# Adapter packs laid out by batch and loaded with eight broadcast loads a block; order of splits in the attention loop changed

## The chip, the cores and the metric

One Trainium2 chip, one core of it, one launch. The time is device microseconds of that core. Every multiplication is done on TensorE (PE); VectorE (DVE), ScalarE (ACT) and GpSimd (POOL) do the elementwise work; SyncE (SP) issues most of the DMA transfers.

## The reference, cut to what matters

Eight sequences of 128 tokens with 512 features, float32, go through four residual blocks. Every sequence (batch entry) b has its own adapter number, so low-rank weights are picked by number at run time.

```
x = x + einsum('bsi,boi->bso', x, W0[lora_ids])                      # block 0: a full matrix per batch entry
# block 1: attention, 32 query heads, 8 key/value heads, head dim 128, rank R = 16
lora_linear(x, w, a, b) = x @ w + (x @ a[ids]) @ b[ids]               # ids = attn_ids
q, k, v = rope(lora_linear(x, wq, aq, bq)), rope(lora_linear(x, wk, ak, bk)), lora_linear(x, wv, av, bv)
p = softmax(q k^T / sqrt(128), causal and masked);  o = p v
x = x + lora_linear(o, wo, ao, bo)
# blocks 2 and 3: rank-16 adapters and one dense 512x512 matrix with bias
```

## The kernel before, in words

Float32 products are made of three matmuls on rounded parts: high x high, high x low, low x high, where high = the value rounded by ScalarE (`ACT.Copy` into the fp32r type) and low = value - high, computed by DVE or POOL. An adapter product needs only rank 16, so the high and low parts are stacked on the partition axis and one matmul with 128 rows does it: for a pair of batch entries the stack holds 4 quarters of 32 rows, each quarter with 16 rows of the even and 16 rows of the odd entry. The "pack" (weight side, `pack0`, `pack1`, written in `split_pieces`, L430, and `low_pieces`, L519) has the high part in partitions 0 to 63 and the low part in 64 to 127. The activation side (`axn`, then transposed to `axt_all`) has high, low, high, low.

The raw rows of a pack come by `load_block_b` (L176): for each of the 8 batch entries SP reads the adapter number into a register and issues 4 loads of 16 rows x 512 columns (32 KB), one for each quarter, 32 loads a block. Five blocks (v 0, v 1, k 0, k 1, and the first query block) are made ahead of the attention loop; the first query block comes from `bq_sel`, a DRAM copy gathered by POOL (L628), by `load_rows` (L180), 4 loads. In the loop `load_bq` (L190) reads the next head's rows, 4 loads for each half.

Phase 1 ("steps" s, 0 to 37, one instruction stream per engine written out by hand): step s does PE `values(s-2)` of block v, `product(s)` of block 0, `adapters(s-1)` and `turn_x1(s)`; ACT and DVE split what these need, in the order of the code. From step 18 on the 16 key units (k) and 4 query units (q) follow: PE `project`, DVE the two rotation products (L609, L611), POOL their sum (L668), SP the store into `k_rot`. PIECES says at which step each piece of a weight block (w) or pack (b) is split. SP's order is one list: x, a, w0 loads of the steps with the block loads between them; a load waits in that list until its buffer is free, and all behind it wait too. `a_raw` has 3 buffers.

Phase 2, the attention loop: 8 key/value heads x 8 slots (one batch entry each). PE in a slot: `scores`, `turn`, `queries`, `outputs` of the entry before last, `values` of the last. In slot 1 of a head ACT makes the 4 high parts of the output weights (`wo_hi`, order 0, 2, `ot`, 1, 3). DVE makes low parts 0 (end of slot 1) and 1 (in slot 2, before the reciprocal), L1004; POOL makes low parts 2 and 3 and that of `ao` (L976, L979). DVE makes the low part of the query pack in every odd slot before the reciprocal (L999). POOL scales the probabilities (L966) and sums the rotation (L959), PE needs the sums of slots 3 and 7 for the scores behind them.

Phase 3, from about 785 us on: blocks 2 and 3.

Of the kernel before, what the change touches and what calls it, by code (L numbers as in the profile page):

```python
# [7 lines left out]
P = 128  # L8
# [18 lines left out]
R_PACK = 16  # L27
# [3 lines left out]
def program(nc, x, xt, lora_ids, pos, attn_ids, slot_ids, mask, w0, wq, wk, wv, wo, a3, bq, bk, bv, ao, bo,  # L31
            l2a, l2b, w3, b3, l3a, l3b, ident_c, causal_c, rope_c, gather_c, twin_c, out):
# [20 lines left out]
    bq_sel = nc.dram_tensor("bq_sel", (B, R, KVH * GW), F32, kind="Internal").ap()  # L53
# [10 lines left out]
    with whole:  # L64
# [30 lines left out]
        twin = sb(whole, "twin", [P, 3])  # L95
        l2b_sel = sb(whole, "l2b_sel", [P, KC, B, R])
# [28 lines left out]
        axn = [sb(early, f"axn{i}", [P, 3, 4, 2, R], F32R) for i in range(2)]  # L125
# [9 lines left out]
        raw_b_in = sem(attn, "raw_b_in")  # L135
# [47 lines left out]
        RAW_B_IN = (512, 1024, 1536, 2048, 2048 + 64)  # L183

# [20 lines left out]
        with ExitStack() as c:  # L205
            for i in (1, 2):
# [5 lines left out]
            RAW = 3  # L212
# [7 lines left out]
                     for flat, at in ((l2a_flat, 0), (l2a_flat, 3 * KC * R), (l2b_flat, 0))]  # L220
# [65 lines left out]
            with nc.Block() as block:  # L286
                @block.sync
                def _(sp):
# [3 lines left out]
                    def load_a(b):  # L292
                        pick = sp.value_load(id_rows[0:1, 1, b:b + 1], min_val=0, max_val=a3.shape[0] - 1)
                        if b >= RAW:
                            sp.wait_ge(a_lo_done, b - RAW + 1)
                        sp.dma_start(a_raw[b % RAW].rearrange("p c n r -> p (c n r)"),
# [24 lines left out]
                    load_block_b(sp, 0)  # L321
                    load_x(1)
                    load_a(1)
                    load_w0(2)
                    load_x(2)
                    load_a(2)
                    for b in range(RAW, B):
                        load_w0(b)
                        load_x(b)
                        load_a(b)  # L330
                        if b == 5:
                            sp.wait_ge(w_lo_done, KC)
                            load_block_w(sp, 1)
                        if b == 6:
                            sp.wait_ge(b_lo_done, PAIRS)
                            load_block_b(sp, 1)
                    sp.wait_ge(b_lo_done, 2 * PAIRS)
                    load_block_b(sp, 2)
# [5 lines left out]
                    load_block_b(sp, 3)  # L344
                    for m in range(VU):
# [29 lines left out]
                def _(act):  # L375
# [21 lines left out]
                    def split_a(b):  # L397
# [3 lines left out]
                        act.activation(a_hi[b % 2][:, :, :, :], a_raw[b % RAW], ACT.Copy).then_inc(a_hi_done, 1)  # L401

                    def pack_hi(b):
# [5 lines left out]
                        act.activation(axn[i][:, :, 0:4:2, i, :], ps_a.unsqueeze(2).broadcast_to([P, 3, 2, R]), ACT.Copy).then_inc(axn_hi_done, 1)  # L409
# [5 lines left out]
                    def split_pieces(s):  # L415
                        for j, kind, k in PIECES.get(s, []):
# [9 lines left out]
                            else:  # L426
                                act.wait_ge(raw_b_in, RAW_B_IN[j])
# [14 lines left out]
                    act.dma_start(ident[:, :], ident_c).then_inc(consts_in, 16)  # L442
                    split_xt(0)
                    split_w0(0, 0, KC)
                    act.wait_ge(consts_in, 16)
# [37 lines left out]
                def _(dve):  # L483
                    low = slice(P // 2, P)
# [19 lines left out]
                    def pack_lo(b):  # L504
                        i = b % 2
                        dve.wait_ge(axn_hi_done, b + 1)
                        dve.tensor_tensor(axn[i][:, :, 1:4:2, i, :], ps_a.unsqueeze(2).broadcast_to([P, 3, 2, R]),
# [1036 lines left out]
```

## Time and profile before

| | us |
|---|---|
| median of 3 runs | 848.53 (847.76 to 848.71) |
| the profiled execution | 849.5 |
| its span in the profile | 847.8 |
| PE busy in the span | 755.8 (89%) |
| DVE, ACT, POOL busy | 536.1, 324.8, 294.1 |
| mean granted clock of PE | 0.956 |

In the rows of the profile a time is the start in us from the begin of the span, then the duration. `SPq` and `ACTq` are the instruction queues that issue transfers. `[16.16 <-DVE res L497]` behind a row means that the engine sat idle for 16.16 us before it and that this wait ended with the named instruction. "x4" merges four instructions into one row.

### The profile page before, as it was taken

The page shows a single profiled execution, that of the slowest core. Times are in us where ns is not written, and L with a number is a line of the kernel's source. Part 1 is how long each engine was busy: PE and PEld are TensorE (multiplying, and loading weights), DVE is VectorE, ACT ScalarE, POOL GpSimd, SP SyncE. Part 2 cuts the span into 40 slices and gives each one's busy share as a digit, 9 for nine tenths or more (in the row PEclk, how much of TensorE's full clock was granted, in tenths as well). Part 3 has the DMA queues.
Part 4 walks back from the last instruction along what each step waited for, and adds up shares of the span by engine and source line. Part 5 has one row for each costly group of instructions (what it writes and reads, how often), then busy time and mean ns, then how long its engine had stood idle before and what let it go on. Part 6 is the DMA issues. An engine that isn't in the chain of part 4 may idle for free. (4 is left out here: it accounts for less than half of the span.)

```text
span 847.8 us, 13367 instructions
## 1 busy us (share of the span) xinstructions
PE 755.8 (89%) x4100; PEld 623.1 (73%) x4100; DVE 536.1 (63%) x1370; ACT 324.8 (38%) x902; POOL 294.1 (35%) x265
## 2 busy tenths in 40 slices
PE   3292989879779999999999999999999999998798
PEld 2282877657567887887887888788788788876586
DVE  3251558756866667657566667666765756654883
ACT  4261525112053435335344435343534533433550
POOL 1020325253545236235326335423623532420220
PEclk8587899989889999999999999999999999999899
DMA  6573678546604122303303302312130310620502
GB/s 218 215 267 94 193 239 269 157 157 191 215 9 137 39 63 66 109 16 108 111 0 108 127 0 62 136 38 62 65 108 21 103 37 0 151 26 2 128 14 87
DMA packets 63083, 87.88 MB, mean 104 GB/s; under 512 B 20086, under 2 KB 37654, under 8 KB 59334
## 3 DMA queue, kind: packets, MB, share of 16 engines
q1 hardware_dynamic: 44338, 73.54, 28.0%
q10 hardware_dynamic: 17044, 8.46, 3.3%
q0 software_dynamic: 1664, 5.44, 2.1%
q8 instruction: 17, 0.28, 0.1%
q14 instruction: 20, 0.16, 0.1%
HBM read 72.45 MB, written 19.68 MB: 109 GB/s over the span
## 5 line engine op out<-in xcount | busy, mean ns | idle before, releaser
L966 POOL TENSOR_TENSOR prob<-prob,rinv 128x512 f32<-128x512 f32 x64 | 66.6, 1040 | 255.3 <-DVE rinv L1054 255.3
L907 ACT ACTIVATE ot_hi<-ps_o 128x512 fp32r<-128x512 f32 x64 | 38.1, 595 | 222.1 <-PE ps_o L1110 222.1
L1122 PE MATMUL ps_out<-wo_hi,ot_hi 128*128 128x512 f32 x256 | 102.8, 402 | 10.4 <-DVE wo_lo L1004 5.7
L959 POOL TENSOR_TENSOR qt<-qc,qs 128x512 f32<-128x512 f32 x60 | 77.9, 1298 | 70.0 <-DVE qs L993 70.0
L917 ACT ACTIVATE prob<-sm,nmax 128x128 f32<-128x128 f32 x256 | 99.8, 392 | 6.2 <-DVE nmax L1035 4.5
L1123 PE MATMUL ps_out<-wo_lo,ot_hi 128*128 128x512 f32 x256 | 101.3, 396 | 0.0
L1124 PE MATMUL ps_out<-wo_hi,ot_lo 128*128 128x512 f32 x256 | 100.8, 394 | 0.0
L78 PE MATMUL ps_q<-x1t_hi,wgt_hi 128*128 128x512 f32 x240 | 100.4, 418 | 0.0
L80 PE MATMUL ps_q<-x1t_hi,wgt_lo 128*128 128x512 f32 x240 | 95.4, 398 | 0.0
L79 PE MATMUL ps_q<-x1t_lo,wgt_hi 128*128 128x512 f32 x240 | 95.2, 397 | 0.0
L1032 DVE MEMSET gate<- 128x1 f32 x64 | 3.8, 59 | 136.9 <-PE ps_s L1091 136.9
L993 DVE TENSOR_TENSOR qs<-ps_q,trig 64x512 f32<-64x512 f32 x120 | 82.6, 689 | 3.7
L1091 PEld LDWEIGHTS ps_s<-kt,qt 128*128 128x128 f32 x512 | 66.6, 193 | 17.5 <-issue 10.3
L1091 PE MATMUL ps_s<-kt,qt 128*128 128x128 f32 x512 | 69.9, 280 | 7.5 <-PEq L286 6.8
L1122 PEld LDWEIGHTS ps_out<-wo_hi,ot_hi 128*128 128x128 f32 x256 | 48.2, 188 | 24.8 <-DVE wo_lo L1004 9.2
L1035 DVE CUSTOM_DVE_ANT_0 sm<-ps_s,maskbias 128x128 f32<-128x128 f32 x256 | 59.1, 286 | 0.9 <-issue 0.2
L1124 PEld LDWEIGHTS ps_out<-wo_hi,ot_lo 128*128 128x128 f32 x256 | 48.0, 187 | 11.6
L901 ACT ACTIVATE pt_hi<-ps_t 128x512 fp32r<-128x512 f32 x64 | 38.2, 596 | 44.1 <-PE ps_t L1100 44.1
L1123 PEld LDWEIGHTS ps_out<-wo_lo,ot_hi 128*128 128x128 f32 x256 | 48.3, 188 | 8.1
L80 PEld LDWEIGHTS ps_q<-x1t_hi,wgt_lo 128*128 128x128 f32 x240 | 45.4, 189 | 10.7
L78 PEld LDWEIGHTS ps_q<-x1t_hi,wgt_hi 128*128 128x128 f32 x240 | 45.8, 191 | 8.0
L79 PEld LDWEIGHTS ps_q<-x1t_lo,wgt_hi 128*128 128x128 f32 x240 | 45.7, 190 | 8.1
(193 smaller groups left out, 1720.2 us busy)
## 6 DMA issues: line engine op xcount, KB each, us to landing
raw_w<-in_wq SPq DMA_DIRECT2D x8, 1024.0 KB, 5.3
wo_raw<-in_wo SPq DMA_DIRECT2D x8, 1024.0 KB, 4.9
raw_b<-bq_sel SPq DMA_DIRECT2D x56, 128.0 KB, 5.2
qt<-in_w SPq DMA_DIRECT2D x5, 1024.0 KB, 6.8
v_hi_d<-v_hi ACTq DMA_DIRECT2D x16, 256.0 KB, 4.6
v_lo_d<-v_lo ACTq DMA_DIRECT2D x16, 256.0 KB, 5.1
kt<-k_rot SPq DMA_DIRECT2D x16, 256.0 KB, 2.6
v_hi<-v_hi_d SPq DMA_DIRECT2D x16, 256.0 KB, 3.2
```

Source lines behind the costliest of these rows:

```text
L78: pe.matmul(bank[:, :], w_hi[:, k, cols], x1t_hi[:, k, tok], start=(k == 0), stop=False)
L79: pe.matmul(bank[:, :], w_hi[:, k, cols], x1t_lo[:, k, tok], start=False, stop=False)
L80: pe.matmul(bank[:, :], w_lo[:, k, cols], x1t_hi[:, k, tok], start=False, stop=False)
L917: e = act.activation(prob[i][:, h, :], sm[:, h, :], ACT.Exp, bias=nmax[i][:, h:h + 1], scale=-1.0, accum_out=rsum[i][:, h:h + 1])
L959: pool.tensor_tensor(qt[:, half, h, :], qc[:, :], qs[:, :], ALU.add).then_inc(q_done, 1)
L966: pool.tensor_tensor(prob[i][:, :, :], prob[i][:, :, :], rinv[i][:, :].unsqueeze(2).broadcast_to([P, G, T]), ALU.mult).then_inc(prob_done, 1)
L993: dve.tensor_tensor(qs[to:to + 64, :], ps_q[i][at:at + 64, :], sin_t[to:to + 64, tok], ALU.mult).then_inc(q_mult, 1)
L1035: m = dve.tensor_tensor_reduce(out=sm[:, h, :], in0=ps_s[i][:, h, :], in1=maskbias[:, b, :], scale=-1.0, scalar=3.0e38, op0=ALU.add, op1=A ...
L1091: mm = pe.matmul(ps_s[b % 2][:, h, :], qt[:, half, h, at:at + T], kt[:, b * T:(b + 1) * T], start=True, stop=True)
L1122: pe.matmul(ps_out[:, :], ot_hi[:, q], wo_hi[:, h, :], start=(h == 0), stop=False)
L1123: pe.matmul(ps_out[:, :], ot_hi[:, q], wo_lo[:, h, :], start=False, stop=False)
L1124: pe.matmul(ps_out[:, :], ot_lo[:, q], wo_hi[:, h, :], start=False, stop=(h == G - 1))
```

## The change

1. Packs are laid out by batch entry: entry b of a pair has partitions 64 (b%2) to 64 (b%2) + 63, in four copies of its 16 rows. One load with a source that repeats four times fills 64 rows (128 KB), so a block takes 8 loads instead of 32. Loads of a pair have their own semaphore.
2. The low part is no longer taken on half of the partitions: one `scalar_tensor_tensor` over 128 partitions computes raw - high where a column of constants (`lows`) is -1 and raw where it is 0. `lows` is one more small constant load on ACT's queue.
3. SP's list: the loads of v block 0 are spread over the steps (pair 0 behind x and a of step 1, pair 1 behind step 2, pairs 2 and 3 behind step 3). `a_raw` has a fourth buffer.
4. `bq_sel` is stored by head, so the gather writes 8 runs of 32 KB per entry.
5. Loop: ACT makes `wo_hi` 0 to 3 in order ahead of `ot`; DVE makes only low part 0, POOL 1, 2 and 3; DVE's query pack low part comes behind the rotation products.

```diff
-    bq_sel = nc.dram_tensor("bq_sel", (B, R, KVH * GW), F32, kind="Internal").ap()
+    bq_sel = nc.dram_tensor("bq_sel", (KVH, B, R, GW), F32, kind="Internal").ap()
...
-        axn = [sb(early, f"axn{i}", [P, 3, 4, 2, R], F32R) for i in range(2)]
+        axn = [sb(early, f"axn{i}", [P, 3, 2, 4, R], F32R) for i in range(2)]
...
-        def load_block_b(dma, j):
+        def load_block_b(dma, j, pairs):
             src = (bv, bv, bk, bk)[j]
             cols = slice(j % 2 * GW, (j % 2 + 1) * GW)
-            for b in range(B):
+            for b in range(2 * pairs[0], 2 * pairs[-1] + 2):
                 pick = dma.value_load(id_rows[0:1, 1, b:b + 1], min_val=0, max_val=src.shape[0] - 1)
-                for quad in range(4):
-                    at = 32 * quad + R * (b % 2)
-                    dma.dma_start(raw_b[at:at + R, b // 2, :], src[bass.DynSlice(pick, 1), :, cols].rearrange("a r n -> (a r) n")).then_inc(raw_b_in, 16)
+                four_times(dma, b, src[bass.DynSlice(pick, 1), :, cols], raw_b_in[b // 2])
+
+        def four_times(dma, b, rows, done):
+            dma.dma_start(raw_b[4 * R * (b % 2):4 * R * (b % 2 + 1), b // 2, :], rows.broadcast_to([4, R, GW])).then_inc(done, 16)
...
         def load_bq(dma, g, h):
-            for quad in range(4):
-                dma.dma_start(raw_b[32 * quad:32 * quad + 32, 2 * h:2 * h + 2, :],
-                              bq_sel.rearrange("(c two) r n -> (two r) c n", two=2)[:, 2 * h:2 * h + 2, bass.DynSlice(g * GW, GW)]
-                              ).then_inc(bq_in[h], 16)
+            for b in range(HALF * h, HALF * (h + 1)):
+                four_times(dma, b, bq_sel[bass.DynSlice(g, 1), b], bq_in[h])
...
                     load_block_w(sp, 0)
-                    load_block_b(sp, 0)
                     load_x(1)
                     load_a(1)
+                    load_block_b(sp, 0, range(0, 1))
                     load_w0(2)
                     load_x(2)
                     load_a(2)
+                    load_block_b(sp, 0, range(1, 2))
                     for b in range(RAW, B):
                         load_w0(b)
                         load_x(b)
                         load_a(b)
+                        if b == 3:
+                            load_block_b(sp, 0, range(2, 4))
...
                             sp.wait_ge(gathered, 2 * B * 16)
-                            load_rows(sp, raw_b, bq_sel[:, :, 0:GW], raw_b_in)
+                            for b in range(B):
+                                four_times(sp, b, bq_sel[0:1, b], raw_b_in[b // 2])
...
-                                act.wait_ge(raw_b_in, RAW_B_IN[j])
+                                act.wait_ge(raw_b_in[k], 32 * (j + 1))
...
-                                dve.tensor_tensor(pack[low, k, :], raw_b[low, k, :], pack[low, k, :].bitcast(F32), ALU.subtract).then_inc(b_lo_done, 1)
+                                dve.scalar_tensor_tensor(pack[:, k, :], pack[:, k, :].bitcast(F32), lows[:, 0:1], raw_b[:, k, :],
+                                                         ALU.mult, ALU.add).then_inc(b_lo_done, 1)
...
-                        pool.dma_start(bq_sel[b:b + 1], bq[pick]).then_inc(gathered, 16)
+                        pool.dma_start(bq_sel[:, b], bq[pick].rearrange("a r (g n) -> (a g) r n", n=GW)).then_inc(gathered, 16)
...
-                        sp.wait_ge(wo_lo_done, G // 2 * (g + 1))
-                        sp.wait_ge(wo_lo_pool, G // 2 * (g + 1))
+                        sp.wait_ge(wo_lo_done, g + 1)
...
-                                wo_hi_part(g, 0)
-                                wo_hi_part(g, 2)
+                                for h in range(G):
+                                    wo_hi_part(g, h)
                             if not first or b >= 1:
                                 ot(t - 1, None if not first else t - 1)
                             if b == 1:
-                                wo_hi_part(g, 1)
-                                wo_hi_part(g, 3)
                                 ao_hi_part(g)
...
-                                for h in range(G // 2, G):
-                                    pool.wait_ge(wo_hi_done, G * g + 2 * (h - G // 2) + 2)
+                                for h in range(1, G):
+                                    pool.wait_ge(wo_hi_done, G * g + h + 1)
                                     pool.tensor_tensor(wo_lo[:, h, :], wo_raw[:, h, :], wo_hi[:, h, :].bitcast(F32),
                                                        ALU.subtract).then_inc(wo_lo_pool, 1)
...
                                 pt(t - 1)
-                            if b == 2:
-                                wo_lo_part(g, 1)
-                            if not last and b % 2:
-                                bq_lo_part(PAIRS * g + b // 2 + 1, b // 2)
                             dve.wait_ge(exp_done, t + 1)
...
                             if not (last and b >= HALF):
                                 rotate(t, (b // HALF + 1) % 2, i)
+                            if not last and b % 2:
+                                bq_lo_part(PAIRS * g + b // 2 + 1, b // 2)
                             if b == 1:
                                 wo_lo_part(g, 0)
```

## Rows read from the trace of the kernel before

**Rows 1.** Page: granted clock of PE in 40 slices of 21.2 us.

```profile
PEclk8587899989889999999999999999999999999899
```

**Rows 2.** Timeline of PE, startup: gaps, and one matmul at either clock.

```profile
41.41 1.12 PE L693 MATMUL ps_x<-ident,res 128*128 128x128 f32 x4 [16.16 <-DVE res L497]
...
85.91 0.90 PE L716 MATMUL ps_ax<-ident_r,axn 128*128 128x128 f32 x3 [16.42 <-DVE axn L507]
...
182.65 0.77 PE L78 MATMUL ps_p<-x1t_hi,wgt_hi 128*128 128x512 f32 x1 [4.89 <-DVE pack L519]
183.21 0.63 PE L79 MATMUL ps_p<-x1t_lo,wgt_hi 128*128 128x512 f32 x1
...
188.71 0.40 PE L80 MATMUL ps_p<-x1t_hi,wgt_lo 128*128 128x512 f32 x1
...
214.97 0.77 PE L78 MATMUL ps_p<-x1t_hi,wgt_hi 128*128 128x512 f32 x1 [2.92 <-DVE pack L519]
```

**Rows 3.** Timeline of SP's queue, startup.

```profile
8.25 1.38 SPq L166 DMA_DIRECT2D raw_w<-in_wv  x1
10.37 19.34 SPq L176 DMA_DIRECT2D raw_b<-in_bv  x32
...
32.43 0.34 SPq L310 DMA_DIRECT2D trig<-in_w  x1
...
63.14 19.05 SPq L176 DMA_DIRECT2D raw_b<-in_bv  x32
...
155.88 19.70 SPq L176 DMA_DIRECT2D raw_b<-in_bk  x32
175.64 0.42 SPq L348 DMA_DIRECT2D k_rot<-l2a_sel  x1
...
202.27 1.83 SPq L180 DMA_DIRECT2D raw_b<-bq_sel  x4
```

**Rows 4.** Timelines of ACT, DVE and POOL, startup.

```profile
20.40 2.18 ACT L425 ACTIVATE wgt_hi<-raw_w 128x512 fp32r<-128x512 f32 x4
37.31 2.00 ACT L391 ACTIVATE wgt_hi<-trig 128x1024 fp32r<-128x1024 f32 x2 [2.27 <-DMA trig<-in_w]
38.40 2.36 DVE L491 TENSOR_TENSOR wgt_lo<-trig,wgt_hi 128x1024 fp32r<-128x1024 f32 x2 [5.87 <-ACT wgt_hi L391]
83.61 0.63 ACT L430 ACTIVATE pack<-raw_b 128x512 fp32r<-128x512 f32 x1 [18.42 <-DMA raw_b<-in_bv]
177.93 1.55 POOL L668 TENSOR_TENSOR l2a_sel<-qt 128x512 f32<-128x512 f32 x1 [13.49 <-DMA k_rot<-l2a_sel]
209.70 2.19 ACT L430 ACTIVATE pack<-raw_b 128x512 fp32r<-128x512 f32 x4 [16.04 <-DMA raw_b<-bq_sel]
```

**Rows 5.** Tile raw_b: durations in ns, min/median/max.

```profile
L176 SPq DMA_DIRECT2D raw_b<-in_bv x64: 315/365/373, 10.4 to 81.8; - x64
L190 SPq DMA_DIRECT2D raw_b<-bq_sel x56: 332/377/768, 225.3 to 657.5; - x56
L999 DVE TENSOR_TENSOR pack<-raw_b,pack x28: 689/689/1472, 247.1 to 710.1; 64x512 fp32r<-64x512 f32 x28
```

**Rows 6.** Busy time by stretch: us, PE PEld DVE ACT POOL, clock, DMA share, GB/s.

```profile
10.00:15.00 5.00, 3.21 (x9) 2.16 (x7) 0.69 (x1) 1.72 (x4) 1.27 (x1) 1.00 0.99 408
140.00:160.00 20.00, 15.01 (x59) 11.75 (x58) 17.72 (x23) 7.83 (x13) 5.47 (x6) 0.91 0.89 276
```

**Rows 7.** Timelines of PE and POOL, slots 1 to 3 of the second head.

```profile
318.64 1.05 PE L1091 MATMUL ps_s<-kt,qt 128*128 128x128 f32 x8
...
328.16 1.05 PE L1091 MATMUL ps_s<-kt,qt 128*128 128x128 f32 x8
...
336.64 1.16 PE L1091 MATMUL ps_s<-kt,qt 128*128 128x128 f32 x8
...
319.89 3.00 POOL L976 TENSOR_TENSOR wo_lo<-wo_raw,wo_hi 128x512 fp32r<-128x512 f32 x2
```

**Rows 8.** PE's wait for the low parts of the output weights, whole span.

```profile
PE ps_out L1122 <- DVE wo_lo L1004: 5.7, 8, 0.9
```

More of the change, by code:

```diff
@@ L31, in program @@
 def program(nc, x, xt, lora_ids, pos, attn_ids, slot_ids, mask, w0, wq, wk, wv, wo, a3, bq, bk, bv, ao, bo,
-            l2a, l2b, w3, b3, l3a, l3b, ident_c, causal_c, rope_c, gather_c, twin_c, out):
+            l2a, l2b, w3, b3, l3a, l3b, ident_c, causal_c, rope_c, gather_c, twin_c, lows_c, out):
     B, T, HID = x.shape
@@ L95, in program @@
         twin = sb(whole, "twin", [P, 3])
+        lows = sb(whole, "lows", [P, 1])
         l2b_sel = sb(whole, "l2b_sel", [P, KC, B, R])
@@ L134, in program @@
         raw_w_in = sem(attn, "raw_w_in")
-        raw_b_in = sem(attn, "raw_b_in")
+        raw_b_in = [sem(attn, f"raw_b_in{p}") for p in range(PAIRS)]
         wq_in = sem(attn, "wq_in")
@@ L219, in program @@
             a_raw = [flat[:, at:at + 3 * KC * R].rearrange("p (c n r) -> p c n r", c=KC, n=3)
-                     for flat, at in ((l2a_flat, 0), (l2a_flat, 3 * KC * R), (l2b_flat, 0))]
+                     for flat, at in ((l2a_flat, 0), (l2a_flat, 3 * KC * R), (l2b_flat, 0), (l2b_flat, 3 * KC * R))]
             kr = [l2a_flat, l2b_flat]
@@ L335, in _ @@
                             sp.wait_ge(b_lo_done, PAIRS)
-                            load_block_b(sp, 1)
+                            load_block_b(sp, 1, range(0, 4))
                     sp.wait_ge(b_lo_done, 2 * PAIRS)
-                    load_block_b(sp, 2)
+                    load_block_b(sp, 2, range(0, 4))
                     sp.wait_ge(w_lo_done, 2 * KC)
@@ L343, in _ @@
                     sp.wait_ge(b_lo_done, 3 * PAIRS)
-                    load_block_b(sp, 3)
+                    load_block_b(sp, 3, range(0, 4))
                     for m in range(VU):
@@ L400, in split_a @@
                             act.wait_ge(ax_ready, b - 1)
-                        act.activation(a_hi[b % 2][:, :, :, :], a_raw[b % RAW], ACT.Copy).then_inc(a_hi_done, 1)
+                        act.activation(a_hi[b % 2][:, :, :, :], a_raw[b % AR], ACT.Copy).then_inc(a_hi_done, 1)
                     def pack_hi(b):
@@ L408, in pack_hi @@
                             act.wait_ge(axt_ready, b - 1)
-                        act.activation(axn[i][:, :, 0:4:2, i, :], ps_a.unsqueeze(2).broadcast_to([P, 3, 2, R]), ACT.Copy).then_inc(axn_hi_done, 1)
+                        act.activation(axn[i][:, :, i, 0:4:2, :], ps_a.unsqueeze(2).broadcast_to([P, 3, 2, R]), ACT.Copy).then_inc(axn_hi_done, 1)
                     def copy_axt(b):
@@ L483, in _ @@
                 def _(dve):
-                    low = slice(P // 2, P)
                     steps = [0]
@@ L579, in _ @@
                     split_w0(0, 0, KC)
+                    dve.wait_ge(consts_in, 32)
                     for s in range(LAST):
@@ L997, in bq_lo_part @@
                         dve.wait_ge(bq_hi_done, n)
[L998 to L1000 removed]
+                        dve.scalar_tensor_tensor(bq_pack[:, p, :], bq_pack[:, p, :].bitcast(F32), lows[:, 0:1], bq_raw[:, p, :],
+                                                 ALU.mult, ALU.add).then_inc(bq_lo_done, 1)
                     def wo_lo_part(g, h):
[L1003 removed]
+                        dve.wait_ge(wo_hi_done, G * g + h + 1)
                         dve.tensor_tensor(wo_lo[:, h, :], wo_raw[:, h, :], wo_hi[:, h, :].bitcast(F32), ALU.subtract).then_inc(wo_lo_done, 1)
@@ L1117, in outputs @@
                             q = slice(h * T, (h + 1) * T)
-                            if b == 0 and h < G // 2:
-                                pe.wait_ge(wo_lo_done, G // 2 * g + h + 1)
+                            if b == 0 and h == 0:
+                                pe.wait_ge(wo_lo_done, g + 1)
                             elif b == 0:
-                                pe.wait_ge(wo_lo_pool, G // 2 * g + h - G // 2 + 1)
+                                pe.wait_ge(wo_lo_pool, (G - 1) * g + h)
                             pe.matmul(ps_out[:, :], ot_hi[:, q], wo_hi[:, h, :], start=(h == 0), stop=False)
@@ L1523, in constants @@
     gather = np.stack([(row % R_PACK == col % R_PACK) & (col // R_PACK % 2 == i) for i in range(2)], 1).astype(np.float32)
-    return {"ident_c": np.eye(P, dtype=np.float32), "causal_c": causal, "rope_c": rope, "gather_c": gather, "twin_c": twin}
+    lows = np.where(np.arange(P)[:, None] % (4 * R_PACK) >= 2 * R_PACK, -1.0, 0.0).astype(np.float32)
+    return {"ident_c": np.eye(P, dtype=np.float32), "causal_c": causal, "rope_c": rope, "gather_c": gather, "twin_c": twin, "lows_c": lows}
 def kernel(**inputs):
```

24 lines of the change are left out of this document (10 added, 14 removed).

## The prediction

> **What bounds the kernel now.** I first read the slices of the page. In the attention loop PE is at 90% or more of every slice and its granted clock is at the upper level; in the first quarter of the span the clock digits fall to 5 and 7 [rows 1]. So the startup (0 to 237 us) has waits of PE that cost twice, once as idle time and once as slow matmuls behind them. PE's timeline shows them: 16.16 us idle before 41.41, 16.42 before 85.91, 4.89 before 182.65, 2.92 before 214.97 [rows 2]. Behind 182.65 the same matmul takes 0.63 us where it takes 0.40 later: 1.2 GHz against 2.4 GHz [rows 2]. Next I asked what SP's queue was doing in these gaps: it was issuing the 32 small loads of an adapter block, for 19.34 us from 10.37, for 19.05 us from 63.14 and for 19.70 us from 155.88 [rows 3]. ACT waits 18.42 us for the second of these blocks (until 83.61), POOL 13.49 us for a k_rot store that stands behind the third, ACT 16.04 us for the first query pack [rows 4]. These loads move 1 MB in 19 us where the DMA engines do 408 GB/s when asked [rows 6]; the issuing, not the moving, takes the time. Of the loop I read slots: 8.48 us from 328.16 to 336.64, but 9.52 from 318.64 to 328.16 [rows 7], the slot in which PE waits for DVE's second low part of the output weights, 8 times in all [rows 8].
>
> **Step 1, the issue time of a block.** One load issues in 0.365 us, and 128 KB loads issue in 0.377 [rows 5], so size does not price it. Per batch entry SP spends 19.34/8 = 2.42 us: four issues of about 0.42 and 0.74 for the register load, as much as lies between the end of raw_w's issue (9.63) and 10.37 [rows 3]. New: 0.74 + 0.42 = 1.16 per entry, 9.3 us a block, 10 less. Bounds of one new issue: 0.33 to 0.77 [rows 5]; I take the median.
>
> **Step 2, the first gap.** PE's wait before 41.41 ends with DVE's addition for step 1, which stands behind DVE's split of w0(2), which waits for the load issued at 32.43 [rows 2 to 4]. New list between raw_w (9.63) and that issue: x(1) 0.4, a(1) 1.1, two pack loads 2.3, register and xt 1.1: issue at about 14.6 instead of 32.43. The DMA engines are full until then, so it lands at some 20 to 23 (1.3 MB at 408 GB/s is 3.2 us, behind 0.5 MB of others). That is in time for ACT, which is busy with the four pieces of raw_w until 22.6 [rows 4]. From there: pack piece 0.6, xt 0.6, two w0 pieces 2.0 (as at 37.31), so 25.8; DVE ends its half 1.45 us after ACT, as 40.76 against 39.31 [rows 4], 27.2; addition 0.7: PE starts at 27.9 instead of 41.41. **13.5 us**. Of the slow matmuls behind the gap (11 x 0.2 us) about half should go, as a gap of 2.7 us stays: **1.0**. Bounds 11 to 15.7.
>
> **Step 3, the second gap.** The second block can't begin earlier than its buffer is free, so everything up to it moves with step 2. ACT needed pair 0 at 65.2 on the old clock of the trace and got the whole block at 83.61 [rows 4]. New: pairs have own semaphores; the loads of pair 0 issue at 63.1 and 64.3 [rows 3], those of pair 1 until 67.0, and land 2 to 5 us later. ACT is then 2 to 6 us late; PE, which could go on until 69.5 (85.91 less 16.42, rows 2), waits 1.6 to 6 us. I take 3.9 us of gap left and 1 us of slow clock instead of 2: 16.4 - 3.9 + 1.0 = **13.5 us**. Bounds 11 to 17.
>
> **Step 4, the v blocks (87 to 155 us).** No gain, no loss. Here DMA is at 0.89 of its time [rows 6] (v stores, gathers), and what ends the waits of ACT is the landing of stores. The change moves no bytes away. It makes the gather of bq write 32 KB runs from 2 KB rows. Bounds: 3 us won, 10 us lost.
>
> **Step 5, the k and q units.** The block issued at 155.88 ends after 9.4 instead of 19.7 us, the store of 175.64 goes out at 165.3, and POOL's wait of 13.49 us shrinks to some 3 [rows 3, 4]. PE has work until 177.8 (182.65 less 4.89), so its gap of 4.89 goes, with 9 slow matmuls behind (1.8 us) and two small stalls after it, 1.9 us as I estimate them. The query pack: issued in 8 x 0.42 = 3.4 us instead of 1.83, but used by pair, so the first pairs come at about the old time; relative to PE, which has won 8.6 us by then, SP's list has won 10.3. The gap of 2.92 goes (and some 2.6 us of slow matmuls, as the clock fell behind it too) [rows 2], sum 14.2. I give 2.7 back: the k_rot stores behind the eight loads land later, and POOL waits for these. **11.5 us**; bounds 6 to 15.
>
> **Step 6, the loop.** PE's extra in slot 2's start is 9.52 - 8.48 = 1.04 us, 8 times, 8.3 us; the row of waits itself says 5.7 [rows 7, 8]. DVE's second low part goes; POOL makes three at 1.5 us each, from 319.9 to 324.4 [rows 7], and `ao` until 325.7. PE, without its stall, needs them at 323.7, 324.4, 325.1 and 325.8: they are in time by 0.1 to 2 us, the last one barely. Then the move of DVE's query low part: the reciprocal and the rotation products come up to 0.7 us earlier in odd slots, and the low part (0.69 us, when against POOL up to 1.47 [rows 5]) now runs beside POOL's rotation sum, on whose end PE's scores wait in slots 4 and 0. The first brings 0.3 us (the products wait for PE's queries), the second costs up to 0.4; 0 to -0.1 net, 15 times, so -1.3. The new low part on 128 instead of 64 partitions costs the same, since a row of 512 elements sets it. **7.0 us**; bounds 2 to 9.5.
>
> By the Trainium skill (SBUF — State Buffer, on the shared port pair) a DVE instruction with two SBUF inputs and a POOL instruction that reads SBUF exclude each other for their whole length. The 1472 ns maximum beside the 689 ns median fits that [rows 5]. By that rule alone each of the 15 meetings would cost the full 0.7 us less the 0.3 won, 6 us, and step 6 would bring 2.
>
> **Small things.** One more constant load on ACT's queue (0.4 us) lies in ACT's wait for the first weights. Three instead of two pieces of POOL in slot 1 end before its next scaling is wanted by PE (328). Phase 3 is untouched.
>
> **Sum.** 14.5 + 13.5 + 0 + 11.5 + 7.0 = 46.5 us. The profiled execution took 849.5, so 803.0; the median is 1.0 lower than that execution, so 802 us.
>
> **The rivals.**
>
> A, the broadcast loads use few DMA engines. If a load whose outermost dimension is the fourfold copy runs on 4 of the 16 engines, 128 KB take 131072/(408/4 GB/s) = 1.28 us [rows 6], a block 10.3 us on these four, and every transfer behind it waits for them. Block 0 is still hidden but for 1 us of step 2. In step 3 pair 1 lands some 3 us later: another 2.5 us. In step 5 the query pack takes 10.3 us and the stores behind it as long: 2.5 more. Time 802 + 6 = 808. For it: nothing in this trace has such a shape, and nothing speaks against it. The Trainium skill (DMA: Bandwidth & Descriptors, the section on why a DMA increments its semaphore by 16) says the count of engines is the largest up to 16 that divides the outermost non-1 sizes of both sides, and its table of mistakes names the leading broadcast; no row here shows it.
>
> B, the v stretch takes back what came earlier: with DMA at 0.89 there, the denser startup leaves a backlog, and the gather in smaller pieces is slower. The bounds of step 4 price it: 10 us, 812. For it: that share. Against it: the two gaps before 87 us are stretches in which DMA does little but these small loads, so the denser startup fills them.
>
> C, slower than before: rival A's four engines, not hidden. Each of the five startup blocks would hold all transfers behind it for 10.3 - 2.6 = 7.7 us, 38 us, and each of the 14 half packs of the loop for 3.8, 53 us, when PE waits for the transfer behind. It decides from 46.5 us on; with all of the startup and 15 us of the loop exposed it gives 802 + 53 = 855. Against it: in the loop a pack has over 60 us before its use.
>
> D, the change doesn't do what it says: the broadcast load issues as slowly as four (0.42 x 4). Then only the new order gains: step 2 some 10, step 6's 7, the pair semaphores 8: 824.
>
> **Chances.** Forecast 0.55, A 0.22, B 0.12, D 0.07, C 0.03; 0.01 for no change. About 0.2% (1.7 us) is what a measurement can tell here. Faster 0.95, same 0.02, slower 0.03. The forecast's own range is 794 to 810; with the best bounds of all steps (15.7 + 17 + 3 + 15 + 9.5 = 60) it would be 789. For 8 in 10 I reach to B and a part of D: 788 to 821.
>
> **What would show it.** Step 1: `raw_b` loads 8 a block, spaced 1.16 us. Step 2: the second `turn_x1` of PE at 28 instead of 41.4. Step 3: a gap of 2 to 6 us before the fourth `turn_ax`. Step 4: the time from there to the last v unit unchanged. Step 5: no PE wait for `pack` over 1.5 us in the k units, store of the first k_rot 10 us after the block's first load. Step 6: slot 2 of a head as long as slot 3, no wait of L1122 for `wo_lo`. Rival A: landing of a pack load over 3 us at an idle DMA, and DMA share low while loads queue. Wrong would be: a v stretch longer by over 10 us, a new wait of PE for POOL in every head, or a gap before 41 us still over 8 us.

## The result, and the profile after

| kernel | median, us | ratio to before [95%] |
|---|---|---|
| before | 848.62 | |
| after | 827.13 (824.06 to 828.97) | 0.974 [0.970, 0.978] |

The change made the kernel 21.5 us faster, where 46.5 us were forecast. The profiled execution took 826.34 us, its span is 824.7. Behind the start of the loop it gave what it should (7.9 us, 7.0 forecast); of the startup's 39.5 us only 15.2 came.

Timeline of PE after, its longest gaps of the startup behind the first steps and the first scores of the loop:

```profile
29.66 1.12 PE L698 MATMUL ps_x<-ident,res 128*128 128x128 f32 x4 [6.26 <-DVE res L500]
...
66.29 0.90 PE L721 MATMUL ps_ax<-ident_r,axn 128*128 128x128 f32 x3 [3.96 <-DVE axn L510]
...
137.94 0.76 PE L78 MATMUL ps_p<-x1t_hi,wgt_hi 128*128 128x512 f32 x1 [4.18 <-DVE pack L522]
...
163.55 0.47 PE L78 MATMUL ps_p<-x1t_hi,wgt_hi 128*128 128x512 f32 x1 [1.80 <-DVE pack L522]
...
203.58 0.77 PE L78 MATMUL ps_p<-x1t_hi,wgt_hi 128*128 128x512 f32 x1 [8.28 <-DVE pack L522]
...
221.74 2.05 PE L1090 MATMUL ps_s<-kt,qt 128*128 128x128 f32 x8 [6.83 <-PEq L285]
```

The two gaps of 16 us are now 6.26 and 3.96, so the order of SP's list does what it should there. But the wait ahead of the query units (of their second, the first that needs all four pieces of the pack) has grown from 2.92 us to 8.28, and the one in front of the second key unit from 3.37 (154.72 in the kernel before) to 4.18. Both end with a low part of a pack. So I read who waits for packs: ACT's high parts of the first query pack, as in the last row of [rows 4].

```profile
187.32 0.63 ACT L433 ACTIVATE pack<-raw_b 128x512 fp32r<-128x512 f32 x1 [13.60 <-DMA raw_b<-bq_sel]
190.05 0.63 ACT L433 ACTIVATE pack<-raw_b 128x512 fp32r<-128x512 f32 x1 [2.10 <-DMA raw_b<-bq_sel]
192.72 0.63 ACT L433 ACTIVATE pack<-raw_b 128x512 fp32r<-128x512 f32 x1 [2.03 <-DMA raw_b<-bq_sel]
195.70 0.63 ACT L433 ACTIVATE pack<-raw_b 128x512 fp32r<-128x512 f32 x1 [2.35 <-DMA raw_b<-bq_sel]
```

SP issued all eight loads between 182.14 and 186.77, 0.58 us apart, yet the pairs land 2.7 to 3.0 us apart: it is no longer the issuing that sets the pace. The table by stretches (columns as in [rows 6]) says what does:

```profile
58.00:63.00 5.00, 4.33 (x28) 3.52 (x26) 2.31 (x4) 0.68 (x2) 0.00 (x0) 1.00 0.27 100
190.00:195.00 5.00, 5.00 (x24) 4.10 (x23) 1.83 (x3) 1.26 (x2) 0.00 (x0) 1.00 0.26 90
```

In these stretches hardly anything but pack loads is under way, ACT waits for them, and still the DMA engines are busy for a quarter: 90 to 100 GB/s, a quarter of the 408 of [rows 6]. That is rival A.

ACT has the last high part at 196.33, but PE starts only at 203.58. What lies between is a k_rot store that SP issued behind the eight loads. It lands 9.4 us later; POOL waits for it, DVE waits for POOL, and DVE's last two low parts stand behind that in its order. The rows are those of SP's queue, POOL and DVE; the last one is the same wait of POOL behind the key block, 13.49 us in [rows 4]:

```profile
186.82 0.49 SPq L350 DMA_DIRECT2D k_rot<-l2b_sel  x1
196.33 1.26 POOL L673 TENSOR_TENSOR l2b_sel<-qt 128x512 f32<-128x512 f32 x1 [8.94 <-DMA k_rot<-l2b_sel]
197.70 0.69 DVE L614 TENSOR_TENSOR qt<-ps_p,trig 128x512 f32<-128x512 f32 x1 [5.80 <-POOL l2b_sel L673]
...
199.86 0.75 DVE L522 SCALAR_TENSOR_TENSOR pack<-pack,lows,raw_b 128x512 fp32r<-128x512 f32 x1
...
202.68 0.75 DVE L522 SCALAR_TENSOR_TENSOR pack<-pack,lows,raw_b 128x512 fp32r<-128x512 f32 x1
...
158.84 1.28 POOL L673 TENSOR_TENSOR l2a_sel<-qt 128x512 f32<-128x512 f32 x1 [10.29 <-DMA k_rot<-l2a_sel]
```

PE was idle from 195.30. With the low part (0.75 us) right behind ACT's last high part it could have gone on at some 197.1, so by this estimate the landing of the pack itself makes about 1.8 of the 8.28 us, and the store behind it the rest.

SP's queue after, then its loads of the k blocks (duration in ns: minimum, median, maximum), then two rows of the DMA issues (the last number is the median from issue to landing):

```profile
11.50 2.68 SPq L179 DMA_DIRECT2D raw_b<-in_bv  x2
...
15.82 0.35 SPq L309 DMA_DIRECT2D trig<-in_w  x1
```

```profile
L179 SPq DMA_DIRECT2D raw_b<-in_bk x16: 615/616/621, 76.6 to 152.2; - x16
```

```profile
qt<-in_w SPq DMA_DIRECT2D x5, 1024.0 KB, 10.5
...
trig<-in_w SPq DMA_DIRECT2D x2, 1024.0 KB, 11.4
```

The third w0 is issued at 15.82 (forecast 14.6, before 32.43). It lands 9.7 us later where it took 4.8 before, at a time when the DMA engines are full (share 1.00 from 12 to 17 us), and PE's row that answers to 41.41 comes at 29.66 and not at 27.9. The 11.4 us is the median of two w0 loads; the other one, issued at 37.1, takes 13.2 us.

### The profile page after: what moved, and what is told of

It reads as the page before. It is cut to its first block and busy times, and to the rows that moved or that the text cites. A ratio compares the mean times of both kernels' runs of the same rounds, so it can differ in the third digit from the quotient of the medians.

```text
span 824.7 us, 13217 instructions
## 1 busy us (share of the span) xinstructions
PE 752.7 (91%) x4100; PEld 624.8 (76%) x4100; DVE 542.7 (66%) x1362; ACT 324.0 (39%) x902; POOL 313.8 (38%) x273
## 5 line engine op out<-in xcount | busy, mean ns | idle before, releaser
L962 POOL TENSOR_TENSOR qt<-qc,qs 128x512 f32<-128x512 f32 x60 | 84.2, 1404 | 78.0 <-DVE qs L995 78.0
L1123 PEld LDWEIGHTS ps_out<-wo_hi,ot_lo 128*128 128x128 f32 x256 | 48.0, 187 | 11.5
L993 DVE TENSOR_TENSOR qc<-ps_q,trig 128x512 f32<-128x512 f32 x60 | 41.4, 690 | 21.2 <-PE ps_q L83 21.2
L78 PE MATMUL ps_p<-x1t_hi,wgt_hi 128*128 128x512 f32 x80 | 35.0, 438 | 18.9 <-DVE pack L522 18.9
## 6 DMA issues: line engine op xcount, KB each, us to landing
qt<-in_w SPq DMA_DIRECT2D x5, 1024.0 KB, 10.5
```

The costliest lines, as they stand in the source:

```text
L78: pe.matmul(bank[:, :], w_hi[:, k, cols], x1t_hi[:, k, tok], start=(k == 0), stop=False)
L962: pool.tensor_tensor(qt[:, half, h, :], qc[:, :], qs[:, :], ALU.add).then_inc(q_done, 1)
L1123: pe.matmul(ps_out[:, :], ot_lo[:, q], wo_hi[:, h, :], start=False, stop=(h == G - 1))
```

## The experiments

Each kernel was timed against the kernel before on the same chip; before took 848.6 to 850.4 us on the chips used. The column of the first scores is the start of the loop in the span of the profiled execution.

| kernel | engines a load | loads a v/k block | median, us | ratio [95%] | first scores |
|---|---|---|---|---|---|
| before | 16 | 32 | 848.62 | | 236.91 |
| after | 4 | 8 | 827.13 | 0.974 [0.970, 0.978] | 221.74 |
| rows outermost | 16 | 8 | 802.23 | 0.945 [0.942, 0.947] | 196.87 |
| small loads | 16 | 32 | 829.65 | 0.976 [0.972, 0.979] | 226.13 |
| two copies | 2 | 16 | 861.24 | 1.013 [1.009, 1.018] | 253.33 |
| old order | 16 | 8 | 807.98 | 0.952 [0.948, 0.956] | 199.89 |
| small rows | 16 | 32 | 842.66 | 0.992 [0.990, 0.994] | 236.06 |
| early packs | 16 | 8 | 798.47 | 0.940 [0.935, 0.945] | 192.19 |
| early packs, again | 16 | 8 | 802.49 | 0.946 [0.943, 0.948] | 188.26 |
| rows outermost, again | 16 | 8 | 803.32 | 0.945 [0.942, 0.948] | 196.12 |
| loop only | 16 | 32 | 843.19 | 0.992 [0.989, 0.994] | |
| output weights only | 16 | 32 | 843.07 | 0.992 [0.990, 0.995] | |

"Engines a load" is rival A's count for the v and k blocks, the outermost extent of the load's rows; it is the thing under test. The query packs of small loads and two copies stay those of the change (4).

**Rows outermost** puts the 16 rows and not the four copies first in source and destination. Bytes, count and order of the loads are those of the change.

```diff
-rows.broadcast_to([4, R, GW])
+rows.rearrange("a r n -> (a r) n").unsqueeze(1).broadcast_to([R, 4, GW])
...
-    lows = -1 where p % 64 >= 32
+    lows = -1 where p % 4 >= 2        # and axn [P, 3, 2, R, 4]
```

> The changed kernel with another order of the rows in a pack: the four copies of a row lie side by side, so the repeating dimension of a load's source is inside the 16 rows and not outside them. Same bytes, same 8 loads a block, same instructions elsewhere. Theory (few engines): in the changed kernel a pack load runs on 4 of 16 DMA engines. Its rows: 90 GB/s at a DMA share of 0.26 from 190 to 195 us, when only pack loads are under way, and pairs that reach ACT 2.7 us apart (190.05, 192.72) although two loads issue in 1.2 us. Then here: pairs land under 1.5 us apart, the issue of a load falls from 0.62 to 0.4 us, the gaps of PE before 66.3, 137.9 and 203.6 shrink by 15 to 20 us in all, total 806 to 814. Rival (issue): SP's queue takes its time for any load of 64 rows, wherever the repetition stands; then issue stays 0.62, total 825 to 829. Rival (DMA-bound startup): bytes decide, total 822 to 829 with a faster landing.

It took 802.23 us, 25 us less than the change and even below the 806 to 814 expected. Two details missed: an issue lasts 0.55 us and not 0.4, and the three gaps named shrink by 7.4 us together (3.96, 4.18 and 8.28 to 0.17, 5.33 and 3.48), not by 15 to 20. The rest came from smaller waits and from the clock: between the row at 29.66 (28.12 here) and the first scores PE is busy for 146.9 us instead of 156.4 for the same matmuls, at a granted clock of 0.96 instead of 0.89. ACT's high parts of the first query pack, the same four as above:

```profile
164.96 0.63 ACT L433 ACTIVATE pack<-raw_b 128x512 fp32r<-128x512 f32 x1 [11.75 <-DMA raw_b<-bq_sel]
166.25 0.63 ACT L433 ACTIVATE pack<-raw_b 128x512 fp32r<-128x512 f32 x1 [0.66 <-DMA raw_b<-bq_sel]
167.45 0.63 ACT L433 ACTIVATE pack<-raw_b 128x512 fp32r<-128x512 f32 x1 [0.57 <-DMA raw_b<-bq_sel]
168.68 0.63 ACT L433 ACTIVATE pack<-raw_b 128x512 fp32r<-128x512 f32 x1 [0.59 <-DMA raw_b<-bq_sel]
```

The pairs come 1.2 to 1.3 us apart, the pace at which SP issues them (5.03 us for the eight). POOL's two waits for k_rot stores, 10.29 and 8.94 us in the change, are 3.90 and 2.54:

```profile
138.19 1.29 POOL L673 TENSOR_TENSOR l2a_sel<-qt 128x512 f32<-128x512 f32 x1 [3.90 <-DMA k_rot<-l2a_sel]
...
169.38 1.29 POOL L673 TENSOR_TENSOR l2b_sel<-qt 128x512 f32<-128x512 f32 x1 [2.54 <-DMA k_rot<-l2b_sel]
```

The other loads of the startup land earlier too:

```profile
qt<-in_w SPq DMA_DIRECT2D x5, 1024.0 KB, 7.8
...
raw_w<-in_wv SPq DMA_DIRECT2D x2, 1024.0 KB, 9.4
raw_b<-in_bv SPq DMA_DIRECT2D x16, 128.0 KB, 3.5
trig<-in_w SPq DMA_DIRECT2D x2, 1024.0 KB, 7.5
```

PE's rows that answer to those of the change, with the 4.18 in front of the second key unit not gone but 5.33:

```profile
55.41 0.55 PE L721 MATMUL ps_ax<-ident_r,axn 128*128 128x128 f32 x3 [0.17 <-DVE axn L510]
...
124.66 0.77 PE L78 MATMUL ps_p<-x1t_hi,wgt_hi 128*128 128x512 f32 x1 [5.33 <-DVE pack L522]
...
196.87 2.05 PE L1090 MATMUL ps_s<-kt,qt 128*128 128x128 f32 x8 [6.84 <-PEq L285]
```

**Small loads**: the change, but the four v and k blocks by 32 loads of 16 rows, in the change's order and with semaphores by pair.

```diff
-four_times(dma, b, src[bass.DynSlice(pick, 1), :, cols], raw_b_in[b // 2])
+for q in range(4):
+    at = 4 * R * (b % 2) + q * R
+    dma.dma_start(raw_b[at:at + R, b // 2, :], src[...].rearrange("a r n -> (a r) n")).then_inc(raw_b_in[b // 2], 16)
```

> The changed kernel, but the loads of the four v and k blocks are again 32 of 16 rows each (the query packs keep the broadcast loads); order in SP's list, semaphores by pair and layout stay changed. Few-engines theory: issuing costs 2.4 us an entry again, 19 us a block, but nothing queues on four engines. The first gap stays small (spread order), the second is 8 to 12 us instead of 4, the k blocks as before: total 828 to 838. If the broadcast loads were harmless, the 5.5 us a block that SP loses more here would show as 10 us and more: total 838 to 846.

829.65 us. Against the change (827.13) the intervals of the two ratios overlap: eight loads on four engines are worth about as much as 32 loads on all. The change's gain in the startup is then in the main that of its order, its semaphores and the fourth buffer. Rows outermost is 27 us below it, by fewer issues or by its query packs; the next kernel was to part these.

**Small rows**: rows outermost, with its query packs, and the v and k blocks by 32 loads. In that layout a load of 16 rows writes every fourth partition.

```diff
-four_times(dma, b, src[...], raw_b_in[b // 2])
+for q in range(4):
+    dma.dma_start(raw_b[at + q:at + 4 * R:4, b // 2, :], src[...].rearrange("a r n -> (a r) n")).then_inc(raw_b_in[b // 2], 16)
```

> Rows outermost (802.2 us), but the four value and key blocks by 32 loads of 16 rows each (every fourth partition); the query packs stay eight loads over all 16 engines. It differs from small loads (829.65 us) in the query packs alone, which there come over 4 engines, and from rows outermost in the count of issues alone. Theory: the 27 us between those two are mostly the issue, 19.7 to 21.2 us a block instead of 10.5; the query packs' part is what PE's wait ahead of the query units differs by, 9.37 against 3.48 us, so about 5. Time 821 to 826 us, first scores of the loop near 219. Rival: the issue is hidden by the order and the semaphores by pair, and most of the 27 us came with the query packs; time 803 to 812 us, first scores before 208.

842.66 us, outside both expectations, as the edit changed a thing that it should not. The loads' durations in ns (minimum, median, maximum), first in small rows and then in small loads:

```profile
L177 SPq DMA_DIRECT2D raw_b<-in_bk x64: 495/538/2202, 86.5 to 176.2; - x64
```

```profile
L177 SPq DMA_DIRECT2D raw_b<-in_bk x64: 315/368/671, 74.9 to 159.3; - x64
```

A load of the same 32 KB issues in 0.54 us instead of 0.37 when it writes every fourth partition, so a block takes SP 25.5 to 27.6 us. It does not part issue and query packs cleanly, but it shows the issue by itself: with the same query packs, 16 us more a block cost 40 us, 2.5 us for each. At that rate the 9 to 11 us a block between small loads and rows outermost are some 24 of their 27 us; that is an estimate, and leaves some 3 for the query packs. PE's wait ahead of the query units says more (9.37 us in small loads, 3.48 in rows outermost, 2.38 in small rows), so the split is open by some 3 us. The fewer issues are worth about as much as the four engines cost, and the change gained the one and paid the other.

**Two copies**: the same question from the other side. Each batch's rows come by two loads of two copies each.

```diff
-dma.dma_start(raw_b[64 rows], rows.broadcast_to([4, R, GW]))
+for half in range(2):
+    dma.dma_start(raw_b[32 rows], rows.broadcast_to([2, R, GW]))
```

> The kernel after, but each batch's rows of the four value and key blocks come by two loads of 64 KB that say each [2 copies][16 rows][512], where it has one of [4 copies][16 rows][512]; places in the pack, order and waits by pair stay, and the query packs too. Bytes are the same, and there are 16 loads a block where the kernel with 32 small loads (829.65 us) has 32. Theory (a load runs on as many DMA engines as its outermost count, and the start of every list falls on the same ones): only 2 of the 16 engines carry these 1 MB, so where nothing else is in flight the DMA share falls from 0.26 to about 0.13 and the rate from 90 to 100 GB/s to about 50; a block drains in some 20.5 us instead of 10.3 us. Issue is 16 x 0.6 + 8 x 0.74 = 15.5 us, so from now on the drain and not the issue sets when a block is there. Between rows-outermost (a block drains in about 2.6 us, 802.2 us) and the kernel after (10.3 us, 827.1 us) the startup lost 3.2 us for each us of drain; by that slope it would be 860 us, by a slope that flattens at least 838 us. The wait ahead of the third turn of the adapter rows (3.96 us in the kernel after) grows past 8 us. Rival (a broadcast source costs per load and not by its engines): the share stays near 0.26 and the time between 825 and 832 us.

861.24 us, slower than the kernel before and near the 860 expected. The stretches of the second key block, in which at the end only pack loads are under way:

```profile
170.00:175.00 5.00, 5.00 (x25) 4.05 (x24) 4.64 (x7) 0.63 (x1) 1.72 (x3) 1.00 0.17 62
175.00:180.00 5.00, 5.00 (x25) 4.14 (x24) 0.75 (x1) 0.63 (x1) 0.00 (x0) 1.00 0.13 49
```

A share of 0.13 is 2 of 16, 49 GB/s is half of the change's. PE's wait for the adapter rows (3.96 us at 66.29 in the change) is 10.91:

```profile
81.70 0.90 PE L724 MATMUL ps_ax<-ident_r,axn 128*128 128x128 f32 x3 [10.91 <-DVE axn L513]
```

For the extents 4 and 2 share and rate go with the outermost extent, and for 16, 4 and 2 the time does: 802, 827 and 861 us. Two copies has 16 loads a block instead of 8, so a part of its loss could be issue; but small loads, with 32 and an issue of the same 20 us a block, is 32 us faster. How many engines a load of rows outermost uses no row shows, since SP's issuing sets its pace; 16 is rival A's count.

**Old order**: rows outermost with all eight loads of v block 0 in the place of before.

```diff
+                    load_block_b(sp, 0, range(0, 4))      # ahead of x(1)
-                    load_block_b(sp, 0, range(0, 1))      # and the other two places
```

> Rows outermost, as in the run of 802.2 us, but the first value block's eight loads are all issued where the kernel before issues its 32, ahead of the second batch's x and adapter load and of the third w0; the semaphores by pair stay. It says what the order of the first block is worth once the loads are spread over all engines. SP then issues 8 x (0.74 + 0.55) = 10.3 us in one piece ahead of x of batch 1, where the kernel before issues for 22.06 us and rows-outermost only 2 loads (2.6 us) ahead of the third w0. Theory that the order matters (the loads of batches 1 and 2 are late by what SP issues ahead of them): the turn of x1 of batch 1 comes near 35 us instead of 28.1 us and the third turn of the adapter rows 4 to 8 us later than at 55.4 us; total 806 to 811 us. Rival (once the issue of a block is 10 us, its place is of no account, since the transfers of the startup fill the 16 engines anyway): first turn later, but all made up by the first key unit (119 to 125 us), total 801 to 804 us.

807.98 us: the order is worth some 6 us (ratio 0.952 [0.948, 0.956] against 0.945 [0.942, 0.947]; against the second timing of rows outermost, [0.942, 0.948], the intervals touch). PE turns x1 of batch 1 at 32.12 us (28.12 in rows outermost; expected near 35), and the loop starts 3.0 us later. In the profiled executions another 4 us lie behind the first scores; no wait that I found accounts for them, and executions of one kernel differ by as much.

**Output weights only** and **loop only** put the loop's edits into the kernel before: first the new split of `wo` alone, then with DVE's query low part behind the rotation too (on 64 partitions, as before).

```diff
-                            if not last and b % 2:
-                                bq_lo_part(PAIRS * g + b // 2 + 1, b // 2)
                             dve.wait_ge(exp_done, t + 1)
...
                                 rotate(t, (b // HALF + 1) % 2, i)
+                            if not last and b % 2:
+                                bq_lo_part(PAIRS * g + b // 2 + 1, b // 2)
```

> As the last, but DVE's low part of the query pack stays ahead of the reciprocal. My step 6 gave 8.3 us to the split of the output weights and -1.3 to the move of the low part: then this is 839 to 841, 1 us faster than the one with both. Rival: the move is what takes PE's wait for the rotation sum away at slots 4 and 0 (3 us in the trace of before): then this is 843 to 845.

> The kernel before with only the edits of the attention loop: wo_hi in order, one low part on DVE and three on POOL, the query pack's low part behind the rotation products (still a subtraction on 64 partitions). The changed kernel's heads are 67.5 us apart instead of 68.8. If that is from these edits alone: 840 to 842. Rival (the loop gains because the pack loads or layout changed): 846 to 849.

843.07 us and 843.19 us. By their ratios and the 850 us of before on that chip, 6.5 and 7.2 us are won, each to within 2.3. The move costs nothing that this measurement can tell; the 1.3 us it was charged with are within the error. Of the expectations, loop only lies above its 840 to 842, and output weights only falls into its rival's 843 to 845. That rival has its cause wrong: PE's weight loads wait for the rotation sum for 3.0 and 3.1 us in the two, 3.1 before, so the move takes nothing away.

**Early packs** is a further version, pointed at by the 5.33 us above. In rows outermost ACT's high parts of the first key block stand in steps 15 to 17, each behind a wait for a v store (3.65 us at 119.28). They move to steps 11 to 13.

```diff
-11: [(2, "w", 0)], 12: [(2, "w", 1)], 13: [(2, "w", 2)], ... 15: [(2, "b", 1)], 16: [(2, "b", 2)], 17: [(2, "b", 3)]
+11: [(2, "w", 0), (2, "b", 1)], 12: [(2, "w", 1), (2, "b", 2)], 13: [(2, "w", 2), (2, "b", 3)]
```

> Rows outermost (802.2 us) and one further edit: the low and high parts of the last three pairs of the first key block are taken in steps 11, 12 and 13 instead of 15, 16 and 17, so that they no longer stand behind ScalarE's waits for the v stores (3.65 us at 119.28) and SP can load the second key block some 15 us earlier. Theory: TensorE's wait of 5.33 us at 124.66 (released by VectorE's low part of a pack) goes to under 1.5 us, and ScalarE's four waits for the loads of the second key block at 129.59 to 137.43 (2.99, 2.02, 1.93, 1.98 us) go to under 0.5; total 796 to 799 us. Rival (the wait is taken back at the query blocks, which wait for the table work and the rotation on VectorE, busy for 7.78 of the 8 us from 172 to 180): total 800.5 to 803 us.

798.47 us. ACT and PE:

```profile
127.01 2.18 ACT L433 ACTIVATE pack<-raw_b 128x512 fp32r<-128x512 f32 x4
```

```profile
121.83 0.50 PE L78 MATMUL ps_p<-x1t_hi,wgt_hi 128*128 128x512 f32 x1 [0.58 <-DVE v_lo L597]
...
174.46 0.47 PE L78 MATMUL ps_p<-x1t_hi,wgt_hi 128*128 128x512 f32 x1 [3.51 <-DVE pack L522]
```

The wait of 5.33 is gone, ACT's four pieces of the second key block run without a wait, and the loop starts 4.7 us earlier. As the interval [0.935, 0.945] meets that of rows outermost, I ran both again on one chip.

> The early packs kernel (798.47 us in its first run) once more, five rounds, beside the next kernel on the same chip. If the edit is worth what the start of the loop showed (4.7 us), it is 3 to 6 us below rows outermost here; if the total gained nothing, within 1.5 us of it.

> Rows outermost once more, five rounds, for the direct comparison with early packs on one chip: 800 to 804 us, 3 to 6 us above early packs if that edit shows in the total.

The profiled executions differ as before, first scores at 188.26 against 196.12 and 796.65 us against 804.55, but the medians are 802.49 (796.65 to 806.25) and 803.32 (798.7 to 806.28). The executions of either kernel spread over about 1%, and the total does not show the gain. Both versions beat the change by 24 to 29 us; between them nothing is decided.

## Why the prediction was wrong

The forecast had the right sign, and the gain came out at less than half of what it named. Its steps against the spans, each stretch as the time won in it (negative: given back). The marks are PE's rows at 85.91 (the fourth turn of adapter rows), at 154.72 (the second key unit) and at 236.91 (first scores) of the kernel before, against 66.29, 137.94 and 221.74 in the change:

```profile
154.72 0.47 PE L78 MATMUL ps_p<-x1t_hi,wgt_hi 128*128 128x512 f32 x1 [3.37 <-DVE pack L519]
...
236.91 2.05 PE L1091 MATMUL ps_s<-kt,qt 128*128 128x128 f32 x8 [6.84 <-PEq L286]
```

| stretch | forecast | after | rows outermost |
|---|---|---|---|
| to 85.91 (steps 2, 3) | 28.0 | 19.6 | 30.5 |
| to 154.72 (step 4) | 0 | -2.8 | -0.4 |
| to 236.91 (step 5) | 11.5 | -1.6 | 10.0 |
| start of the loop | 39.5 | 15.2 | 40.0 |
| behind it (step 6) | 7.0 | 7.9 | 8.6 |

**The step that failed is the choice between the forecast and rival A, and A's price.** The prediction knew the mechanism, with its 1.28 us a load and 10.3 us a block, gave it 0.22, and charged 6 us. In the sum, the step furthest off is step 5: it gave back 2.7 us for k_rot stores that land behind the eight loads, and took POOL's wait of 13.49 us to shrink to some 3; it is 10.29, and 11.5 us forecast became -1.6. The cause is shown: between the change and rows outermost only the order of the dimensions differs, with the places of the copies in the pack that follow from it, and it holds 25 us, of which 24.9 are there at the start of the loop (221.74 less 196.87). The chance was set by what this trace did not show; the only statement that bore on the shape was the Trainium skill's (DMA: Bandwidth & Descriptors, the section on why a DMA increments its semaphore by 16). The traces agree with it: a share of 0.26 for an outermost 4 in the change, 0.13 for a 2 in two copies.

The price fell short in three places. *Steps 2 and 3*: 8.4 us missing where A had 3.5. A counted how late the pack itself lands. But the block's loads also hold the 1 MB loads issued behind them: the w0 load issued at 37.1 takes 13.2 us to land, its like in rows outermost 6.4. Between the rows at 29.66 and 66.29 PE thus has two more waits (1.41 and 1.74 us) and is busy for 29.5 us, 27.1 in rows outermost, at a granted clock of 0.87 instead of 0.94. *Step 4*: 2.8 given back, within its bounds; A had nothing. *Step 5*: 13.1 us missing where A had 2.5. A had the right path, the stores behind the pack loads, at too low a price. Of the 8.28 us ahead of the query units, some 6.5 are the store that POOL and with it DVE's low parts waited for, and only some 1.8 the pack itself, by the estimate above; POOL's 10.29 us behind the key block is the same path: the block's eight loads take SP 13.76 us to issue, and the store behind them lands 5.8 us later. In rows outermost the two waits are 3.90 and 2.54. The 4.18 ahead of the second key unit is not A's: rows outermost has 5.33 there, behind ACT's waits for v stores. The sum priced as "all exposed" under rival C was 38 us for the startup; 25 us of it came true, and of the loop's 53 next to nothing (8.6 us won behind the first scores in rows outermost, 7.9 in the change).

Of the 24.9 us at the start of the loop 9.5 are slower matmuls (156.4 less 146.9 us busy) and the rest idle time: the waits cost twice here too, as the prediction said of the kernel before.

**Step 1** forecast 1.16 us an entry. Rows outermost needs 1.31 (10.5 us a block), the change 1.72 (13.75 at 76.64): an issue lasts 0.62 us in its blocks and 0.55 in rows outermost, where the median of one new issue was put at 0.42. The bounds held 0.62; the row taken as nearest (0.377) has the same size and not the same shape. Small rows shows that the shape prices an issue: 0.54 against 0.37 at one size. But the order of the dimensions alone does not: the loads of the query packs issue in 0.55 us in both kernels. What makes the rest of the 1.72, 1.1 us beside the issue where rows outermost has 0.76, is open.

**Step 2** (13.5 at the row of 41.41, and 1.0 of clock behind it): 11.75 at that row in the change, 13.3 with the first cause taken away (28.12). **Step 3**: the gap that stays was put at 3.9 and is 3.96; in rows outermost it is 0.17. The forecast's gap came out right by luck: it had the pack too late and no narrow loads, and the two errors cancelled there.

**Step 6** is right, in its mechanism too. Slot 2 takes 8.38 us (303.52 to 311.90) where it took 9.52, as long as slot 3 (311.90 to 320.28):

```profile
303.52 1.05 PE L1090 MATMUL ps_s<-kt,qt 128*128 128x128 f32 x8
...
311.90 1.05 PE L1090 MATMUL ps_s<-kt,qt 128*128 128x128 f32 x8
...
320.28 1.05 PE L1090 MATMUL ps_s<-kt,qt 128*128 128x128 f32 x8
```

POOL makes the three low parts in 3.80 us, 1.27 each, faster than the 1.5 assumed, so they are in time; of PE's 5.7 us of waiting [rows 8] no row is left, and its weight loads wait 0.3 us in the whole span:

```profile
305.50 3.80 POOL L978 TENSOR_TENSOR wo_lo<-wo_raw,wo_hi 128x512 fp32r<-128x512 f32 x3
309.27 1.28 POOL L981 TENSOR_TENSOR ao_pack<-ao_raw,ao_pack 128x512 fp32r<-128x512 f32 x1
```

The moved query low part does meet POOL, and more than forecast: it takes 1886 ns in the median, 689 before, and POOL's rotation sum 1404 ns in the mean, 1298 before. PE hardly feels it: it waits 0.9 us for that sum in the whole span, and its weight loads 1.7 where they waited 3.1 before:

```profile
L1000 DVE SCALAR_TENSOR_TENSOR pack<-pack,lows,raw_b x28: 752/1886/1896, 234.6 to 690.1; 128x512 fp32r<-128x512 f32 x28
```

```profile
L1090 PE MATMUL ps_s<-kt,qt 128*128 128x128 f32 x512 | 69.0, 278 | 8.2 <-PEq L285 6.8 <-POOL qt L962 0.9
```

So the rule of the Trainium skill on the shared port pair (SBUF — State Buffer) agrees with the trace in the durations; the 5 us that it would have taken from step 6 don't come, since the meeting lies off PE's path.

**Rivals B and D.** The v stretch took back 2.8 us, not 10, and 0.4 in rows outermost. One load does not issue as slowly as four (0.62 us, not 1.7). B's 812 has neither the cause nor the size. D's 824 lies near the measured time by chance: small loads has the issue time that D assumed and the new order, and took 829.65.

## What to carry to other kernels

Ahead of folding many small loads into one, write down the outermost extent of its source and destination: extents of 2, 4 and 16 took 861, 827 and 802 us here, for the same bytes. Put the long dimension outermost and let the repeated one follow; where a layout must be chosen anyway, choose it for that. Fewer issues are worth their time only while SP's list is what PE waits for: here 2.5 us of the total for each us of issue in a block, with four such blocks. Price a narrow load by what it holds up behind it in the queues, not by its own landing, and read it off a profile as a DMA share that stays at a quarter while somebody waits. Here most of the longest wait was a 256 KB store issued behind the narrow loads, two engines away from the one that stood idle: follow such a wait to its start before putting it down to the tile that it names.

## What the runs showed of the hardware that I had not expected

Loads of [4][16][512] from one copy of the rows kept 0.26 of the DMA engines busy (90 to 100 GB/s) with several of them under way, those of [2][16][512] 0.13 (49 GB/s): successive loads did not spread over other engines. A 256 KB store issued behind eight of the first kind landed after 9.4 us, behind eight of [16][4][512] after 2.6. A DVE operation of 512 elements a row that ran beside POOL's took 1886 ns instead of 752. The issue of a load on SP goes by its shape in the v and k blocks: 0.37 us for 16 rows to 16 neighbouring partitions, 0.54 for the same rows to every fourth, 0.62 with four copies outermost and 0.55 with the rows outermost for the same 128 KB. For the query packs it took 0.55 in either order, so the order is not all of it.
